# Expert down projection of a ViT block: FP32 matmuls replaced by three FP32R products of high and low parts, groups interleaved with the up projection

## The reference, cut to what matters here

```python
logits = xf @ Wr.T + br                       # xf: 2080 x 128, eight experts
comb   = top-2 of softmax(logits), zero elsewhere
h = gelu(einsum('nd,edh->enh', xf, W1) + b1)  # up: hidden 256
o = einsum('enh,ehd->end', h, W2) + b2        # down: back to 128
y = einsum('ne,end->nd', comb, o)
```

## Time and profile before

| | |
|---|---|
| median of three runs | 276.25 us (274.6 to 277.44) |
| profiled execution, its own time | 276.12 us |
| its span, first to last instruction | 274.3 us |
| mean granted TensorE clock over the span | 0.985 of full |
| PE busy, share of the span | 89% |
| VectorE, ScalarE, GpSimd busy | 60%, 47%, 22% |

### The profile page before, as it was taken

One profiled execution on the slowest core, in us unless ns is written; L12 is line 12 of the kernel. 1 busy time (PEld: TensorE's weight loads), 2 busy tenths in 40 slices (PEclk: granted clock), 3 DMA queues, 4 the chain that ended last, 5 costly groups with the idle time before them and its releaser, 6 DMA issues.

```text
span 274.3 us, 6405 instructions
## 1 busy us (share of the span) xinstructions
PE 243.3 (89%) x2519; PEld 209.3 (76%) x2519; DVE 163.9 (60%) x512; ACT 129.6 (47%) x432; POOL 60.5 (22%) x77
## 2 busy tenths in 40 slices
PE   0799997999886888895799978999999999999993
PEld 0665564899674656675689966999999999999993
DVE  0476888635679999999689463333333324242453
ACT  1543057942487999960015794052526262626100
POOL 8930122292023443563027000000000000000000
PEclk9999999999999999999999996899999999999998
DMA  6960000000000000270000000000000000000015
GB/s 218 279 142 2 1 0 0 2 4 2 0 0 4 2 2 2 88 223 5 5 2 0 4 0 0 2 0 0 2 0 0 2 1 2 0 4 0 0 25 133
DMA packets 6554, 7.95 MB, mean 29 GB/s; under 512 B 833, under 2 KB 5295, under 8 KB 6396
## 3 DMA queue, kind: packets, MB, share of 16 engines
q1 hardware_dynamic: 5260, 6.32, 8.2%
q10 hardware_dynamic: 720, 0.87, 1.2%
q0 software_dynamic: 544, 0.35, 0.5%
HBM read 6.47 MB, written 1.06 MB: 27 GB/s over the span
## 4 chain that ended last, share of the span: by engine, by line
PE 61%; DVE 24%; ACT 4%; DMA 4%; issue 3%; POOL 2%; ACTq 0%; DVEq 0%
PE banks L987 56%; DMA region_d<-in_L_tok_W_sw 4%; DVE stb L720 3%; DVE top L736 3%; DVE stb L640 2%; ACT region_d L510 2%; DVE stats L625 2%; DVE xnT L833 2%; PE banks L1186 2%; DVE region_c L761 2%; POOL rstd L309 2%; DVE mv L628 1%; DVE h L616 1%; DVE ntop L743 1%; DVE tmpx L828 1%
## 5 line engine op out<-in xcount | busy, mean ns | idle before, releaser
L977 DVE SCALAR_TENSOR_TENSOR KT<-banks,vbd,KT 128x128 f32<-128x128 f32 (+1 forms) x136 | 38.0, 344 | 61.1 <-PE banks L987 61.1
L510 ACT ACTIVATE region_d<-banks,vecs 128x416 f32<-128x416 f32 x80 | 45.6, 611 | 55.2 <-PE banks L987 55.2
L987 PE MATMUL banks<-w_all,region_d 128*128 128x128 f32 (+1 forms) x544 | 64.1, 278 | 0.0
L987 PEld LDWEIGHTS banks<-w_all,region_d 128*128 128x128 f32 (+1 forms) x544 | 62.2, 190 | 1.6 <-issue 0.6
L488 ACT ACTIVATE region_e<-banks,ntop 128x64 f32<-128x64 f32 x128 | 38.2, 326 | 7.0 <-DVE rsum L754 3.5
L987 PE MATMUL banks<-x_hi,w_hi 128*128 128x416 f32 x80 | 29.9, 373 | 0.9 <-ACT region_d L510 0.9
L987 PE MATMUL banks<-x_lo,w_hi 128*128 128x416 f32 x80 | 28.6, 358 | 0.0
L987 PE MATMUL banks<-x_hi,w_lo 128*128 128x416 f32 x80 | 28.6, 357 | 0.0
L488 ACT ACTIVATION_READ_ACCUMULATOR region_e<-banks,ntop 128x1 f32 x128 | 27.9, 218 | 0.0
L343 POOL TENSOR_TENSOR region_e<-region_e,rsum 128x512 f32<-128x512 f32 (+1 forms) x16 | 16.5, 1032 | 37.3 <-DVE rsum L754 37.3
L987 PEld LDWEIGHTS banks<-x_hi,w_hi 128*128 128x128 f32 x80 | 15.3, 191 | 2.8 <-issue 1.4
(11 more groups left out here) (219 smaller groups left out, 381.5 us busy)
## 6 DMA issues: line engine op xcount, KB each, us to landing
region_a<-in_x SPq DMA_DIRECT2D x2, 512.0 KB, 6.2
region_a<-in_x SPq DMA_DIRECT2D x1, 1024.0 KB, 11.0
w_sb<-in_L_ffn_W SPq DMA_DIRECT2D x1, 1024.0 KB, 5.6
out<-KT SPq DMA_DIRECT2D x8, 128.0 KB, 2.4
region_d<-in_L_attn_rel_v SPq DMA_DIRECT2D x2, 260.0 KB, 9.8
kc<-in_consts ACTq DMA_DIRECT2D x1, 336.0 KB, 5.7
region_d<-in_L_tok_eps_in ACTq DMA_DIRECT2D x2, 128.0 KB, 7.5
region_d<-in_L_tok_W_w ACTq DMA_DIRECT2D x1, 128.0 KB, 7.9
```

The costliest lines, as they stand in the source:

```text
L510: a.activation(HB[:, e % 2, s, blk * FB:(blk + 1) * FB], bank[h_bank(i)][:, 0:FB], ACT.Gelu, bias=vecs[:, v:v + 1]).then_inc(S["gelu_ok"], 1)
L977: last = v.scalar_tensor_tensor(acc[0:m, t, :], bank[out_bank(u)][0:m, i * C:(i + 1) * C], comb[0:m, t, e:e + 1], acc[0:m, t, :], op0=ALU. ...
L987: return t_.matmul(o, l, r, start=start, stop=stop)
```

## The change

Experts 0 and 1 (`e < SPLIT`, with `SPLIT = 2`) keep the plain FP32 down projection. For experts 2 to 7:

- the gelu values are kept as a high part `HBH` (rounded to FP32R) and a low part `HBL` (exact minus high), and W2 as `w2_hi` and `w2_lo`. `down` issues three FP32R matmuls in place of each FP32 one: high x high, high x low, low x high. The stationary operand is still the tile of 128 tokens, the moving one still 128 columns.
- ScalarE computes the gelu twice from PSUM, once into `HBH` and once, exact, into a ring of five buffers `GX` (a view of `region_e`). For two of the ten pieces of an expert (`shared`: the second hidden half of blocks 1 and 3) VectorE makes the high part instead, by a copy.
- GpSimd subtracts the two to make `HBL` (ten instructions of 416 columns per expert), and makes `w2_lo` in pieces of 256 columns (`split2`).
- ScalarE makes `w2_hi` in one copy of 1536 columns, behind `w1_hi`.
- the waits follow: `down` waits for `hlo_ok` and `w2lo_ok` in place of `gelu_ok`; a gelu into the ring waits for the subtraction five pieces back; a piece of expert e waits for the group of expert e - 2 with its own number.

For all experts TensorE's order becomes `down(e, g)`, `up(e + 2, g)`, group by group. Buffers move in SBUF to make room: the early regions are given back, and `HBH`, `HBL`, `combs` and the parts of W2 are laid over them.

```diff
 pe:
-                pe.wait_ge(S["gelu_ok"], 10 * e + 2 * need)
+                if e < SPLIT:
+                    pe.wait_ge(S["gelu_ok"], 10 * e + 2 * need)
+                else:
+                    pe.wait_ge(S["w2lo_ok"], e - SPLIT + 1)
+                    pe.wait_ge(S["hlo_ok"], 10 * (e - SPLIT) + 2 * need)
...
-                        last = mm(bank[out_bank(u)][0:m, i * C:(i + 1) * C], HB[:, e % 2, s, t * P:t * P + m],
-                                  w2_sb[:, e, s, :], s == 0, s == 1)
+                        if e < SPLIT:
+                            last = mm(o, HB[:, e % 2, s, t * P:t * P + m], w2_sb[:, e, s, :], s == 0, s == 1)
+                        else:
+                            hi, lo = (h[:, e % 2, s, t * P:t * P + m] for h in (HBH, HBL))
+                            mm(o, hi, w2h[:, e - SPLIT, s, :], s == 0, False)
+                            mm(o, hi, w2l[:, e - SPLIT, s, :], False, False)
+                            last = mm(o, lo, w2h[:, e - SPLIT, s, :], False, s == 1)
...
             for e in range(E):
                 for g in range(5):
                     down(e, g)
-                if e + 2 < E:
-                    for blk in range(5):
-                        up(e + 2, blk)
+                    if e + 2 < E:
+                        up(e + 2, g)
 scalar:
+            act.wait_ge(S["d_ffn"], 16)
+            act.wait_ge(S["w1_ps"], 8)
+            a.activation(w2_hi[:, :], w2_tail, ACT.Copy).then_inc(S["w2hi_ok"], 1)
...
+                if s == 0:
+                    act.wait_ge(S["y2_ps"], 5 * (e - 2) + blk + 1)
+                n = i - 10 * SPLIT
+                if not shared(i):
+                    a.activation(HBH[:, e % 2, s, b], h, ACT.Gelu, bias=bias)
+                if n >= NX:
+                    act.wait_ge(S["hlo_ok"], n - NX + 1)
+                a.activation(GX[n % NX], h, ACT.Gelu, bias=bias).then_inc(S["gelu_ok"], 1)
 gpsimd:
+            split2(SPLIT)
+            for e in range(SPLIT, E):
+                for i in range(10 * e, 10 * e + 10):
+                    hidden_low(i)
+                    if i == 10 * e + 4 and e + 1 < E:
+                        split2(e + 1)
 vector, behind the four or one accumulations of (e, g):
+                    i = 10 * (e + 2) + 2 * g - 1
+                    if e + 2 < E and g > 0 and shared(i):
+                        hidden_high(i)
```

More of the change, by code:

```diff
@@ L35 @@
 FB = ALL // 5
+SPLIT = 2
+NX = 5
 K_ID, K_PE, K_E8, K_VM, K_E8T = 0, 128, 256, 384, 512
@@ L92, in vit_kernel @@
         ident = kc[:, K_ID:K_ID + P]
[L93 to L106, removed]
         QT = sb("QT", ALL)
@@ L118, in vit_kernel @@
         OTc = sb("OTc", IMG)
[L119 to L122, removed]
         stb = sb("stb", 1024)
@@ L175, in vit_kernel, with passing @@
         rs_ = sb("rs_", 2 * NT)
-        combT = vbd[:, 0:5 * P]
-        combP = vbd[:, 5 * P:10 * P]
-        comb = combP.rearrange("p (t e) -> p t e", e=32)
         early = ExitStack()
+        def passing(name, cols):
+            return early.enter_context(nc.sbuf_tensor(name, [P, cols], F32))
+        region_c = passing("region_c", PJ * IMG * QC)
+        PT = region_c[:, :].rearrange("p (j b q) -> p j b q", j=PJ, b=IMG)
+        gate = region_c[:, 2 * TOK:3 * TOK]
+        region_d = passing("region_d", 2 * 2 * ALL)
+        QP = region_d[:, 0:2 * TOK].rearrange("p (j b q) -> p j b q", j=2, b=IMG)
+        QPf = region_d[:, 0:2 * TOK].rearrange("p (j t) -> p j t", j=2)
+        HB = region_d[:, :].rearrange("p (u s t) -> p u s t", u=2, s=2)
+        pc_rep = region_d[:, 0:TOK].rearrange("p (r h d) -> p r h d", r=PAIRS, h=H)
+        wprep = region_d[:, 0:1024].rearrange("p (w i) -> p w i", w=4)
+        ei = region_d[:, 1024:1536]
+        ei_root = region_d[:, 1536:2048]
+        ei_sign = region_d[:, 2048:2560]
+        wn = region_d[:, 2560:3072].rearrange("p (w i) -> p w i", w=2)
+        rvd = region_d[:, 3072:3072 + QC * HD].rearrange("p (q d) -> p q d", q=QC)
+        vbd = passing("vbd", IMG * C)
+        VBD = vbd[:, :].rearrange("p (b c) -> p b c", b=IMG)
+        RVBD = passing("RVBD", QC * 32)
+        RV = RVBD[:, :].rearrange("p (q s d) -> p q s d", q=QC, s=2)
         region_a = early.enter_context(nc.sbuf_tensor("region_a", [P, 8192], F32))
@@ L188, in vit_kernel @@
         early.close()
+        HBL, HBH = (ctx.enter_context(nc.sbuf_tensor(n, [P, 4 * ALL], F32R))[:, :]
+                    .rearrange("p (u s t) -> p u s t", u=2, s=2) for n in ("hb_lo", "hb_hi"))
+        combs = sb("combs", 10 * P)
+        combT = combs[:, 0:5 * P]
+        combP = combs[:, 5 * P:10 * P]
+        comb = combP.rearrange("p (t e) -> p t e", e=32)
+        w2_hi, w2_lo = (ctx.enter_context(nc.sbuf_tensor(n, [P, (E - SPLIT) * FH], F32R)) for n in ("w2_hi", "w2_lo"))
+        w2h, w2l = (w[:, :].rearrange("p (e s d) -> p e s d", s=2, d=C) for w in (w2_hi, w2_lo))
+        sb("between", IMG * C + QC * 32 - 10 * P - 2 * (E - SPLIT) * FH)
+        GX = [region_e[:, FB * i:FB * i + FB] for i in range(NX)]
         w1_sb = sb("w1_sb", E * FH)
         w2_all = sb("w2_all", E * 2 * C)
+        w2_tail = w2_all[:, SPLIT * FH:E * FH]
         w2_sb = w2_all[:, :].rearrange("p (e s d) -> p e s d", e=E, s=2)
@@ L203, in vit_kernel @@
         w2_ps o_ok oc_ok op_ps opc_ps h1_ok h1a_ok h1c_ok ve2_ok rstd2_ok xn2_ok x2T_ps x2T_ok  lg_ps
-        lg_ok lexp_ok comb_ok cT_ps cT_ok base_ps acc_ok h_ps gelu_ok y2_ps h0o_ok relkb_ok dve_c dve_m act_c
+        lg_ok lexp_ok comb_ok cT_ps cT_ok base_ps acc_ok h_ps gelu_ok y2_ps h0o_ok relkb_ok w2hi_ok w2lo_ok hhiD_ok hlo_ok dve_c dve_m act_c
         pool_c""".split()
@@ L368, in _, with split2 @@
             deviation2(4)
+            def split2(e):
+                w = slice((e - SPLIT) * FH, (e - SPLIT + 1) * FH)
+                if e == SPLIT:
+                    pool.wait_ge(S["w2hi_ok"], 1)
+                g.tensor_tensor(w2_lo[:, w], w2_tail[:, w], w2_hi[:, w].bitcast(F32), ALU.subtract)\
+                    .then_inc(S["w2lo_ok"], 1)
+            def hidden_low(i):
+                e, s, blk = i // 10, i % 2, (i // 2) % 5
+                n = i - 10 * SPLIT
+                b = slice(blk * FB, (blk + 1) * FB)
+                pool.wait_ge(S["gelu_ok"], i + 1)
+                if shared(i):
+                    pool.wait_ge(S["hhiD_ok"], 2 * (e - SPLIT) + blk // 2 + 1)
+                g.tensor_tensor(HBL[:, e % 2, s, b], GX[n % NX], HBH[:, e % 2, s, b].bitcast(F32), ALU.subtract)\
+                    .then_inc(S["hlo_ok"], 1)
+            split2(SPLIT)
[4 more added lines that the diff above has]
+                        split2(e + 1)
         @block.scalar
@@ L506, in gelu @@
                 act.wait_ge(S["h_ps"], i + 1)
[L507 to L511, removed]
+                b = slice(blk * FB, (blk + 1) * FB)
+                bias = vecs[:, V_FB1 + 2 * e + s:V_FB1 + 2 * e + s + 1]
+                h = bank[h_bank(i)][:, 0:FB]
+                if e < SPLIT:
+                    a.activation(HB[:, e % 2, s, b], h, ACT.Gelu, bias=bias).then_inc(S["gelu_ok"], 1)
+                    return
+                if s == 0:
+                    act.wait_ge(S["y2_ps"], 5 * (e - 2) + blk + 1)
+                n = i - 10 * SPLIT
+                if not shared(i):
[3 more added lines that the diff above has]
+                a.activation(GX[n % NX], h, ACT.Gelu, bias=bias).then_inc(S["gelu_ok"], 1)
             for n in (2, 3):
@@ L968, in _ @@
                 base(u)
+            def hidden_high(i):
+                e, s, blk = i // 10, i % 2, (i // 2) % 5
+                n = i - 10 * SPLIT
+                dve.wait_ge(S["gelu_ok"], i + 1)
+                v.tensor_copy(HBH[:, e % 2, s, blk * FB:(blk + 1) * FB], GX[n % NX]).then_inc(S["hhiD_ok"], 1)
             for e in range(E):
@@ L1362, in down @@
                     m = P if t < PAIRS else IMG
+                    o = bank[out_bank(u)][0:m, i * C:(i + 1) * C]
                     for s in range(2):
-                        last = mm(bank[out_bank(u)][0:m, i * C:(i + 1) * C], HB[:, e % 2, s, t * P:t * P + m],
-                                  w2_sb[:, e, s, :], s == 0, s == 1)
+                        if e < SPLIT:
+                            last = mm(o, HB[:, e % 2, s, t * P:t * P + m], w2_sb[:, e, s, :], s == 0, s == 1)
[4 more added lines that the diff above has]
+                            last = mm(o, lo, w2h[:, e - SPLIT, s, :], False, s == 1)
                 last.then_inc(S["y2_ps"], 1)
```

## The result

The kernel with the change takes 295.8 us (median of four runs, 295.59 to 300.7) against 276.85 us before: ratio 1.0697, 95% interval 1.0648 to 1.0745. It is slower by 19 us.

A forecast was written before the change was run, and what follows sets the result against it. TensorE, start to start, was taken to bound the experts' stage. To 276.1 us came +21.0 (down, experts 2 to 7), +1.6 and -0.8 (changes from down to up), sum +21.8: 298 us, range 287 to 318.

The forecast's parts named there:

- load-bound case: Down projection, experts 2 to 7: each full-tile FP32R record costs its weight load, 0.1115 us; 290 to 308 us, chance 72%.
- the larger of 0.058 (stream) and 0.1115 (load): Cost of a 128-column FP32R matmul in the down projection: stream or load, whichever is larger, so 0.1115 us.
- the row it is nearest to: The FP32 down record, 0.1115 us from start to start, taken as nearest match for the 128-column FP32R record.
- 8 more changes at 0.2 = +1.6 us: Experts 0 and 1: interleaving adds 8 changes from FP32 down to up, each a 0.2 us pause; +1.6 us.
- the -0.8: Experts 2 to 5: going from FP32R down to FP32R up, each loses its one change pause; -0.8 us.
- the 0.1 us of stalls per down projection: Down projection, experts 2 to 7: stalls as now, 0.1 us, included in the 11.2 us per expert.
- Hidden work: ScalarE 10.4, GpSimd 10.8 and VectorE's copies under 1 us per expert stay under TensorE's 16.9 us period; cost 0.
- Load not bare: Down projection: FP32R loads overlap more freely or are short, so a matmul costs 0.058 us; 266 us, chance 10%.
- Operand loaded once: Down projection: the repeated high part is loaded once, two loads for three matmuls, 0.223 us a product; 277 us, chance 4%.
- The matmul waiting for its whole load: Down projection: each matmul waits for its whole load, 0.19 us each; +67 us, 343 us, chance 4%.
- Feeding: Experts' stage: VectorE's adds and GpSimd's subtractions take turns, delaying four experts by 1 to 4 us; 302 to 314 us, 7%.
- The clock: Load-bound stretch: TensorE's granted clock could drop to 1.2 GHz; 30 us or more, chance 3%.

The follow-up runs named there:

- fp32_interleaved: The kernel before with only the new group-by-group order of down and up, all down projections staying FP32; 276.22 us, ratio 1.0.
- half_load: The kernel after, with only the first 64 tokens of each 128-token tile as stationary operand in down of experts 2 to 7; 269.67 us.
- wide: The kernel after, with both products of the high gelu part in one matmul of 256 moving columns, so two matmuls per half; 275.9 us.
- two_products: The kernel after without the product of high gelu and low W2 in experts 2 to 7; 273.86 us.
- swap: The kernel after with down operands exchanged in experts 2 to 7: W2 stationary, 416 tokens moving, output left transposed; 264.72 us.

## Why the prediction was right

Direction, mechanism and size held: 298 us forecast, 295.8 measured, inside the 290 to 308 of the load-bound case and the stated range of 287 to 318. One term of the sum was wrong, and is told below.

**The record.** The central step, "the larger of 0.058 (stream) and 0.1115 (load)", measured 0.111 us in the kernel after and 0.060 us with half the load. What it rested on, two FP32R loads 0.11 us apart after a pause, was a sound reading: that is the time for which a load holds its path, and the 0.19 us of its record include latency.

The other support, FP32 records of 128 columns at 0.1115 us as "the row it is nearest to", says less about the load than it seems to. The last two FP32 records of an expert start 0.11 us apart as well (193.67 and 193.78 us), and they load only 32 columns, in 109 ns; in FP32R the same tile goes at 0.06. So an FP32 record of 128 moving columns would cost 0.11 us for its stream alone, and it fits that one of 512 columns costs 0.43. The agreement of FP32 and FP32R at 0.11 is in part chance. The rows that carry the argument are the two loads after the pause and the router's, with 8 moving columns.

**Experts 2 to 5.** Forecast 16.9 us a period, measured 16.79; +3.18 each instead of +3.3, 12.7 us together.

**Experts 6 and 7.** From the first to the last record after, (294.19 - 272.14) / 2 = 11.0 us each; before, (269.74 - 254.26) / 2 = 7.74. +3.28 each, 6.6 us together, where 3.5 was forecast.

**Experts 0 and 1.** This is the term that was wrong. "8 more changes at 0.2 = +1.6 us" came out as -0.25 us: 14.60 and 13.57 us against 14.80 and 13.61. Most of the -0.25 is expert 0, which runs partly at the low clock and takes 14.4 to 15.1 us in the traces with the same FP32 work, so no effect of the change can be read from it. The pause of 0.2 us in the earlier trace rows was laid on the change from down to up. It belongs to the FP32 tile of 32 tokens that comes just before it, as fp32_interleaved shows with 24 more changes for nothing. The trace before already had it: the prediction counts "each of the six changes", but from 186 us on there are five. The sixth pause stands between the down projections of experts 6 and 7, with no up matmul near:

```profile
254.07 7.78 PEld L987 LDWEIGHTS banks<-w_all,region_d 128*128 128x128 f32 x68
262.05 7.70 PEld L987 LDWEIGHTS banks<-w_all,region_d 128*128 128x128 f32 x68 [0.20 <-issue]
```

In the experts with FP32R the pause is gone altogether, which the -0.8 had right for the wrong reason. Why an FP32 tile of 32 tokens brings a pause is open.

The sum is 12.7 + 6.6 - 0.25 = 19.0 us, against 19.2 in the profiles and 18.95 in the medians. The forecast of 21.8 was too high by 1.85 us in experts 0 and 1 and by 0.9 us in the six others (four times 0.12, twice 0.22). In those the 0.1 us of stalls per down projection did not recur; the rest is rounding.

**Hidden work.** ScalarE and GpSimd were forecast at 10.4 and 10.8 us per expert, and are 9.5 to some 11.5; a subtraction measured 1081 ns, not 1.0 us. VectorE's two copies, forecast at under 1 us per expert, took 0.84 us in experts 2 and 3 and 1.23 in experts 4 to 7. The copy of `w2_hi` took 1.48 us at 125.8 us, in ScalarE's idle time. All free, as said.

**The rivals.** Load not bare: half_load and wide rule it out. Operand loaded once: two_products and the equal counts of PE and PEld. The matmul waiting for its whole load: starts at 0.11 and not 0.19. Feeding: swap reaches 11.3 us without a hole, and the adds of 128 columns take 344 ns after as against 345 before, beside a busy GpSimd. The clock: 1.00 in both windows above.

The Trainium skill gives 81 ns for a load and a matmul of 128 columns ("TensorE: Matmul & The Clock Gate", "Back-to-back issue gap"). That does not hold for FP32R here, which takes 111. By the same page's section "LDWEIGHTS (loading the stationary operand)" a load of 128 columns takes an estimated 128 / 1.2 = 107 ns, and the traces agree with that, with loads 0.11 us apart.

## What to carry to other kernels

Before an FP32 matmul is split into cheaper products, price each product as the larger of its stream and its weight load. With 128 stationary columns an FP32R record cost 0.11 us at 128 moving columns, though its stream needs 0.06. Three products lost with 128 columns moving (+19 us) and gained with 416 (swap, -11 us, a part of it by the exchange alone). If the narrow side must move, the number of loads is the cost; put more columns behind one load, or drop a product if the precision allows it. And before a pause is laid on a change from one kind of work to another, look for a place in the trace where it stands without that change. Here one of the six did.

## What the runs showed of the hardware that was not expected

A VectorE copy from SBUF to SBUF and a GpSimd subtraction keep each other waiting even at this small size. The copy of 416 columns (L1032) takes 0.36 to 0.87 us in the kernel after and 0.35 to 1.29 us in swap. In swap it takes 0.83 us when it starts at 217.74 us, inside a pair of subtractions that ends at 218.33:

```profile
216.70 1.13 DVE L1042 SCALAR_TENSOR_TENSOR KT<-banks,combs,KT 128x128 f32<-128x128 f32 x4 [1.12 <-PE banks L1055]
217.74 0.83 DVE L1032 CAST hb_hi<-region_e 128x416 fp32r<-128x416 f32 x1
...
221.48 0.35 DVE L1032 CAST hb_hi<-region_e 128x416 fp32r<-128x416 f32 x1
```

```profile
216.20 2.13 POOL L404 TENSOR_TENSOR hb_lo<-region_e,hb_hi 128x416 fp32r<-128x416 f32 x2
...
221.50 1.29 POOL L404 TENSOR_TENSOR hb_lo<-region_e,hb_hi 128x416 fp32r<-128x416 f32 x1
```

At 221.48 us the copy came first, and the subtraction that started beside it took 1.29 us instead of about 1.07. The four adds at 216.70 us, which read PSUM and one operand in SBUF, ran beside the same subtractions in 1.13 us, as in the earlier trace rows. So the adds are free of GpSimd, as forecast, and the copy is not, a wait that the prediction did not price; it costs nothing here because VectorE has room.
